# Four graph layers on one core: the tail of the neighbour maximum, with x fetched again, row minima, sums and statistics placed otherwise

## The reference, cut to what matters

```python
# x: (8192, 128) float32; adj: (8192, 8192) int32 of 0 and 1, symmetric, ones on the diagonal
def _L0_gnn_ref(X, adj):            # maximum over the neighbours, feature by feature
    neg = finfo(float32).min
    vals = max over j of where(adj[i, j] != 0, X[j, :], neg)
    return where(any(adj[i] != 0), vals, 0)

x = _layernorm(x + _L0_gnn_ref(x, adj))        # layer 0
x = _layernorm(x + attention_1(x, W1, a1, adj)) # layers 1 to 3: masked softmax attention
x = _layernorm(x + attention_2(adj, x, W2, a2))
x = _layernorm(x + attention_3(x, adj, W3, a3))
```

## Time and profile before

| what | value |
|---|---|
| median of three runs | 5988.77 us (5978.95 to 5993.84) |
| profiled execution: time / span | 6010.32 us / 6008.3 us |
| mean granted TensorE clock | 0.922 of full speed |
| busy share: PE, DVE, ACT, POOL | 84%, 79%, 34%, 20% |
| last `take_top` (L571) ends | 2253.55 us |
| first instruction of layer 1 on VectorE (L930) | 2316.70 us |

### The profile page before, as it was taken

One profiled execution on the slowest core, in us unless ns is written; L12 is line 12 of the kernel. 1 busy time (PEld: TensorE's weight loads), 2 busy tenths in 40 slices (PEclk: granted clock), 3 DMA queues, 4 the chain that ended last, 5 costly groups with the idle time before them and its releaser, 6 DMA issues. The chain is left out here.

```text
span 6008.3 us, 91716 instructions
## 1 busy us (share of the span) xinstructions
PE 5075.2 (84%) x24003; PEld 2392.2 (40%) x24113; DVE 4748.3 (79%) x8829; ACT 2028.6 (34%) x2862; POOL 1186.8 (20%) x1368
## 2 busy tenths in 40 slices
PE   4777767667677674899999999979999998999999
PEld 3333333333333332344444444435444445444444
DVE  6676766667666665699989998988888886888888
ACT  3444444444444441555555555510000001000000
POOL 5555454454444540000000000000000000000000
PEclk6888888888888885999999999998999998999999
DMA  7555555555555522011111111011222211221211
GB/s 256 191 189 190 188 187 180 178 189 187 184 185 181 184 94 85 29 43 44 44 43 43 44 44 44 29 44 63 72 76 74 73 49 71 74 82 67 89 60 35
DMA packets 149498, 628.30 MB, mean 105 GB/s; under 512 B 29360, under 2 KB 37936, under 8 KB 91632
## 3 DMA queue, kind: packets, MB, share of 16 engines
q1 hardware_dynamic: 78432, 482.58, 23.0%
q0 software_dynamic: 33744, 73.21, 4.1%
q10 hardware_dynamic: 36864, 67.13, 3.2%
HBM read 551.42 MB, written 75.56 MB: 104 GB/s over the span
## 5 line engine op out<-in xcount | busy, mean ns | idle before, releaser
L1258 PE MATMUL bank<-w,GX 128*128 128x512 f32 x6144 | 2777.6, 597 | 41.9 <-DVE w L1489 22.3
L1258 PEld LDWEIGHTS bank<-w,GX 128*128 128x128 f32 x6144 | 1145.6, 190 | 1398.2 <-issue 1340.4
L1503 DVE SCALAR_TENSOR_TENSOR w<-q,E,m 128x512 f32<-128x512 f32 x2048 | 1455.0, 758 | 170.0 <-PE bank L1258 92.0
L306 POOL DMA_INDIRECT ring<-x_ext,idx x1051 | 1030.4, 980 | 1098.1 <-DVE X L560 338.4
L450 PE MATMUL sums<-lone,xs 128*128 128x512 fp8e4 x3000 | 852.3, 427 | 300.9 <-DVE top L548 204.3
L548 DVE TENSOR_TENSOR top<-top,sums 128x1024 f32<-128x1024 f32 x484 | 589.8, 1219 | 645.2 <-remote 378.2
L375 ACT ACTIVATE stage<-tp 128x1024 fp8e4<-128x1024 uint16 x512 | 523.9, 1025 | 1089.9 <-remote 634.7
L1478 DVE SCALAR_TENSOR_TENSOR u<-theta,E,m 128x512 fp8e4<-128x512 f32 x1024 | 765.9, 749 | 98.3 <-issue 84.9
L1322 ACT ACTIVATE above<-bank,offset 128x512 fp8e4<-128x512 f32 x1024 | 649.0, 684 | 529.3 <-PE bank L1187 527.0
L1489 DVE SCALAR_TENSOR_TENSOR w<-q,E,u 128x512 f32<-128x512 f32 x1024 | 760.6, 744 | 74.9 <-PE bank L1258 74.8
L450 PEld LDWEIGHTS sums<-lone,xs 128*128 128x128 bf16 x3000 | 295.2, 106 | 827.4 <-issue 619.0
(11 more groups left out here) (231 smaller groups left out, 3018.2 us busy)
## 6 DMA issues: line engine op xcount, KB each, us to landing
adjb<-in_adj SPq DMA_DIRECT2D x256, 1024.0 KB
m<-mask_t SPq DMA_DIRECT2D x192, 1024.0 KB, 4.9
mask_t<-stage ACTq DMA_DIRECT2D x256, 256.0 KB
ring<-x_ext,idx POOLq DMA_INDIRECT x1051
out<-X SPq DMA_DIRECT2D x16, 256.0 KB, 2.4
Wn<-in_L_gnn_W SPq DMA_DIRECT2D x3, 64.0 KB, 1.9
A<-in_L_gnn_a SPq DMA_DIRECT2D x6, 0.5 KB, 2.1
X<-in_x SPq DMA_DIRECT2D x4, 0.5 KB, 22.3
```

The costliest lines, as they stand in the source:

```text
L306: pool.indirect_dma_start(ring[:, s, :], None, x_ext, bass.IndirectOffsetOnAxis(ap=idx[:, k, s:s + 1], axis=0)).then_inc(done, 16)
L1258: last = nc.tensor.matmul(acc[b][:, :], GX[:, j, :], w[:, j % WR, :], start=(j == 0), stop=(j == T - 1))
L1503: nc.vector.scalar_tensor_tensor(out=w[:, j % WR, :], in0=q, scalar=E[:, j:j + 1], in1=m[:, b, j, :], op0=ALU.max, op1=ALU.mult).then_inc( ...
```

## The change

- SyncE fetches x a second time as soon as the last adjacency tile has been turned, into `adjb` (`x_again`); `xin` and `bn0` go.
- The row minima of quads 0 to 14 are taken one quad at a time, one behind each of pairs 8 to 22 of the last quad; that of quad 15 behind the last `take_top`.
- GpSimd adds `x_again` to quads 0 to 14 of `nm`, one instruction a quad, behind its last gather; VectorE adds quad 15.
- The 64 `bn_stats` and 64 `bn_aggr` come before the branch, in the same block. ScalarE makes the flag of the reduced value. `first_norm` and its block go; the product with the 0/1 flag, with another sum and another set of statistics, stands in the branch that is not taken.
- The fallback's `tmp` moves from `adjb` to the second half of `stage[:, 0]`; `lowest` is a part of `codes`, `bn` a part of `keys`.

```diff
+LOWEST_AT = 8
+    nohas = found
-        tmp = adjb[:, :, :].rearrange("p h n -> p (h n)").bitcast(F32)[:, 0:FJ * F]
+        tmp = stage[:, 0, :, :].rearrange("p a b -> p (a b)").bitcast(F32)[:, FJ * F:2 * FJ * F]
+        x_again = adjb[:, :, :].rearrange("p h n -> p (h n)").bitcast(F32).rearrange("p (t f) -> p t f", f=F)
+        lowest = codes[:, 0:T]
+        bn = keys[:, 0:6 * T].rearrange("p (t s) -> p t s", s=6)
...
+            sp.wait_ge(transposed, T * 8)
+            sp.dma_start(x_again, x.rearrange("(t p) f -> p t f", p=P)).then_inc(x_back, 16)
             sp.wait_ge(flag_ready, 1)
...
             report()
+            pool.wait_ge(x_back, 16)
+            for quad in range(NC - 1):
+                at = slice(quad * TC, (quad + 1) * TC)
+                pool.wait_ge(rows_step, quad + 1)
+                nc.gpsimd.tensor_tensor(out=nm[:, at, :], in0=nm[:, at, :], in1=x_again[:, at, :], op=ALU.add).then_inc(x_added, 1)
             pool.wait_ge(missed_ready, 1)
...
                 act.wait_ge(stage_out[q], NC // 2 * STORES * 16)
+            act.wait_ge(missed_shared, 1)
+            nc.scalar.activation(flag[:, :], missed_all[:, :], ACT.Copy).then_inc(flag_ready, 1)
...
+            def lowest_of(quad):
+                at = slice(quad * TC, (quad + 1) * TC)
+                rows_done.did(nc.vector.tensor_reduce(lowest[:, at], nm[:, at, :], axis=AXX, op=ALU.min))
+            def between(n):
+                if n == LOWEST_AT:
+                    dve.wait_ge(top_used, NC - 1)
+                    dve.wait_ge(lower_free, T - TC + 1)
+                    dve.wait_ge(rest_free, T - TC + 1)
+                if LOWEST_AT <= n < LOWEST_AT + NC - 1:
+                    lowest_of(n - LOWEST_AT)
+            def row_statistics():
+                rows_done.settle()
+                dve.wait_ge(x_added, NC - 1)
+                for t in range(T):
+                    rows_done.did(nc.vector.bn_stats(bn[:, t, :], nm[:, t, :]))
+                rows_done.settle()
+                for t in range(T):
+                    rows_done.did(nc.vector.bn_aggr(stats[:, t, :], bn[:, t, :]))
+                rows_done.settle()
...
                     if quad is not None:
                         pair(quad * 32 + 8 * k + e, 8 * k + e, quad == NC - 1)
+                    if quad == NC - 1:
+                        between(8 * k + e)
...
-            dve.wait_ge(lower_free, T + 1)
-            dve.wait_ge(rest_free, T + 1)
             merge(NC - 1)
             take_top(NC - 1)
             dve.wait_ge(top_used, NC)
-            lowest = junk
-            steps.do(nc.vector.tensor_reduce(lowest, nm[:, :, :], axis=AXX, op=ALU.min))
             steps.did(nc.vector.scalar_tensor_tensor(out=due[:, :], in0=due[:, :], scalar=TOP_BIT, in1=found[:, :], op0=ALU.mult, op1=ALU.not_equal))
+            lowest_of(NC - 1)
+            rows_done.settle()
+            dve.wait_ge(x_back, 16)
+            last = slice(T - TC, T)
+            rows_done.did(nc.vector.tensor_tensor(out=nm[:, last, :], in0=nm[:, last, :], in1=x_again[:, last, :], op=ALU.add))
...
             nc.vector.tensor_reduce(missed[:, :], due[:, :], axis=AXX, op=ALU.max).then_inc(missed_ready, 1)
-            dve.wait_ge(missed_shared, 1)
-            nc.vector.tensor_copy(flag[:, :], missed_all[:, :]).then_inc(flag_ready, 1)
+            steps.do(nc.vector.tensor_scalar(nohas[:, :], deg[:, :], 0.0, None, ALU.is_equal))
+            row_statistics()
             dve.wait_ge(flag_ready, 1)
...
-            neighbour_max(...)
-            first_norm(nc, x, X, deg, nohas, stats)
+            neighbour_max(...)
```

More of the change, by code:

```diff
@@ L208, in neighbour_max @@
         x_copied = sem("x_copied")
+        x_back = sem("x_back")
+        rows_step = sem("rows_step")
+        x_added = sem("x_added")
         split = sem("split")
@@ L571, in take_top @@
                 nc.vector.tensor_tensor(out=tiles, in0=tiles, in1=turned_ps, op=ALU.max).then_inc(top_used, 1)
+            rows_done = Steps(dve, rows_step)
+            def lowest_of(quad):
[17 more added lines that the diff above has]
+                rows_done.settle()
             def phase(t, k, extracts=True, finishes=True, quad=None, tops=True):
@@ L704, in _ @@
             dve.wait_ge(top_used, NC)
-            lowest = junk
-            steps.do(nc.vector.tensor_reduce(lowest, nm[:, :, :], axis=AXX, op=ALU.min))
+            steps.settle()
+            side.settle()
             steps.did(nc.vector.scalar_tensor_tensor(out=due[:, :], in0=due[:, :], scalar=TOP_BIT, in1=found[:, :], op0=ALU.mult, op1=ALU.not_equal))
+            lowest_of(NC - 1)
[3 more added lines that the diff above has]
+            rows_done.did(nc.vector.tensor_tensor(out=nm[:, last, :], in0=nm[:, last, :], in1=x_again[:, last, :], op=ALU.add))
             steps.do(nc.vector.scalar_tensor_tensor(out=lowest, in0=lowest, scalar=0.0, in1=deg[:, :], op0=ALU.is_le, op1=ALU.mult))
@@ L743, in _ @@
                     hold(dve, fb_adj_used, t + 2)
-def first_norm(nc, x, X, deg, nohas, stats):
-    with ExitStack() as ctx:
-        sem = SEMS[0]
-        bn = ctx.enter_context(nc.sbuf_tensor("bn0", [P, T, 6], F32))
-        xin = ctx.enter_context(nc.sbuf_tensor("xin", [P, T, F], F32))
-        x_in, step, bn_done, ag_done = sem("x_again"), sem("step0"), sem("bn_done"), sem("ag_done")
-        block = ctx.enter_context(nc.Block())
-        @block.sync
-        def _(sp):
-            sp.dma_start(xin[:, :, :], x.rearrange("(t p) f -> p t f", p=P)).then_inc(x_in, 16)
-        @block.vector
-        def _(dve):
-            s = Steps(dve, step)
-            s.do(nc.vector.tensor_scalar(nohas[:, :], deg[:, :], 1.0, None, ALU.min))
-            s.do(nc.vector.tensor_tensor(out=X[:, :, :], in0=X[:, :, :], in1=nohas[:, :].unsqueeze(2).to_broadcast([P, T, F]), op=ALU.mult))
-            s.do(nc.vector.tensor_scalar(nohas[:, :], nohas[:, :], -1.0, 1.0, ALU.mult, ALU.add))
-            dve.wait_ge(x_in, 16)
-            s.do(nc.vector.tensor_tensor(out=X[:, :, :], in0=X[:, :, :], in1=xin[:, :, :], op=ALU.add))
-            for t in range(T):
-                nc.vector.bn_stats(bn[:, t, :], X[:, t, :]).then_inc(bn_done, 1)
-            dve.wait_ge(bn_done, T)
-            for t in range(T):
-                nc.vector.bn_aggr(stats[:, t, :], bn[:, t, :]).then_inc(ag_done, 1)
-            dve.wait_ge(ag_done, T)
+                rows_done.did(nc.vector.tensor_scalar(lowest, nohas[:, :], -1.0, 1.0, ALU.mult, ALU.add))
+                rows_done.settle()
+                rows_done.did(nc.vector.tensor_tensor(out=nm[:, :, :], in0=nm[:, :, :], in1=lowest.unsqueeze(2).to_broadcast([P, T, F]), op=ALU.mult))
+                rows_done.settle()
+                rows_done.did(nc.vector.tensor_tensor(out=nm[:, :, :], in0=nm[:, :, :], in1=x_again, op=ALU.add))
+                row_statistics()
 def attention_layer(nc, layer, W, a_src, a_dst, mask_t, X, nohas, stats, rstd, ident, lastrow, dest, out=None):
```

## The result

The changed kernel takes 5957.78 us (median of 5 executions, 5947.05 to 5960.98); the kernel before took 5987.64 us beside it (5 executions, 5978.95 to 5993.84). The ratio is 0.9949, 95% interval 0.9938 to 0.996: **29.9 us less**. The forecast was 5955.9 us, 32.9 less. The profiled execution took 5960.48 us, its span is 5957.5 us, its mean granted TensorE clock 0.928.

The account below looks back on a forecast made before the run. The prediction took a plain chain on VectorE, 63.15 us behind take_top, as the bound; 39.7 less 3.3 (minima) less 3.5 (collisions) gave 32.9 us off 5988.8, so 5955.9 us, range 5944 to 5974.

Parts of the forecast that it names:

- The chain: From the end of take_top to layer 1: 23.4 us in place of 63.15, 39.7 us less.
- the jump: VectorE's branch passing over 130 more instructions behind the statistics: 1.0 us for a code fetch, bounds 0 and 2.
- Ten minima: Minima between pairs 13 and 23 on VectorE: 3.3 us late at pair 23, bounds 0 and 10.35.
- Collisions of folds and sums: VectorE's folds of ring meeting GpSimd's sums: half of nine lose 0.78 us each, 3.5 us, bounds 0 and 11.7.
- Five minima for nothing: Minima behind pairs 8 to 12, ahead of the 5.64 us wait in front of pair 13: cost nothing.
- The fetch: Second fetch of x, issued at about 2157 us: some 22 us long, landing near 2180, cost 0.
- GpSimd's sums: Fifteen sums of 1.155 us from 2216.56, after 9.19 idle, ending at about 2243; their own length hidden.
- Rival 4: GpSimd's sums set the end: cost starts at 3.1 us each; at 6.6 us each the time is 6008 us; 3%.
- The drain: GpSimd's 8.4 us drain behind its reduction at the block's end: covered by VectorE's statistics, costing nothing.
- Rival 1: Drain belongs to the block's end, not the reduction, and is uncovered: 6.85 to 8.4 us lost, 5964 us; 8%.
- Rival 3: TensorE's clock falls to the 1.2 GHz level for pairs 14 to 31: 22.7 us come back, 5979 us; 4%.
- another layout of code: An example of effects the prediction could not see that would make the kernel slower: 1%.

Follow-up runs that it names:

- second set: Follow-up runs e6 to e9, on a chip of their own, where the kernel before stands at 5457.75 us (9 executions).
- e7: Changed kernel with 230 repeated waits, never executed, in VectorE's fallback branch, and a few on other engines; 5436.71 us, 0.9962 of before.
- e10: As e7 but with 266 waits instead of 230, 18 instructions more in VectorE's list; 5479.77 us (1 execution).
- e3: Changed kernel without the minima of quads 0 to 14, GpSimd's sums no longer held for them; 5433.08 us (1 execution).
- e9: Changed kernel with no edit, run again on another chip; 5437.01 us (5 executions), 0.9965 of before.
- e4: Changed kernel with the 128 statistics instructions moved behind the branch into a block of their own; 5510.62 us (1 execution).
- e2: Changed kernel with all 64 tiles' sums on VectorE in one instruction behind the last take_top, none on GpSimd; 5432.86 us (1 execution).
- e1: Kernel before with no edit, profiled a second time; 5464.39 us (1 execution).
- e5: Kernel before with GpSimd's reduction over partitions replaced by a copy; 5456.79 us (1 execution).
- e6: Changed kernel with x fetched twice, one behind the other, into the same place; 5432.28 us (1 execution).
- e8: Changed kernel with minima, GpSimd's sums and checks moved, 64 bn_aggr made six instructions, and 460 waits padding the branch; 5427.0 us, 0.9942 of before.

## Why the prediction was right

The forecast of 5955.9 us stands against 5957.78, inside the range, and faster by 0.5%. The mechanism, a plain chain of which 40 us go, was right. That the total came within 2 us is in part luck: the same change brings 20.7 us in the second set, and several terms below are off in ways that the first comparison hides or evens out. By its own steps:

- **The chain.** 23.4 forecast, 22.44 measured; 39.7 less, 40.7 measured. The one term that was off is the jump, put at 1.0 (bounds 0 and 2): it cost 0.4 in the changed kernel (0.6 from branch to drain, 0.2 before), and 2.5 more, outside the bounds, in e7 and e10, whose branch is longer still. 130 more instructions could be passed for next to nothing, 244 could not.
- **Ten minima.** 3.3 forecast, 3.8 by e3 against e9, 4.8 against e4.
- **Collisions of folds and sums.** 3.5 forecast, as half of nine folds losing 0.78 each; the four rows grew by 3.63, but as seven folds losing 0.52 on average, so the number is right by another mix. e2 has 4.9 to 5.9 for all that the sums did to pairs 13 to 23. The two terms together: 6.8 forecast, 6.9 in the first pair of traces. By e2 and e3 it would be 8.7 to 10.7. The kernel before itself takes 21.8 us in this stretch in e1 and 18.2 in e5, so the split into two terms is good to a couple of us, no better, and the 6.9 of one pair of traces is no closer confirmation than that. The Trainium skill (SBUF — State Buffer, "Who interferes with whom") spares instructions with one SBUF input, and the trace agrees: pairs and minima kept their 1.21 and 0.68 us beside the sums.
- **Five minima for nothing.** This rested on the wait of 5.64 us ahead of pair 13, and it holds where that wait is. In the first pair of traces pairs 8 to 12 take 19.5 and 19.7 us: the five minima fill VectorE's idle time, which falls from 10.2 to 7.7 us. The wait itself stayed (it is 6.39 after, and ends with `remote`, for something that the profile doesn't name); it was the idle time between the pairs that shrank. On the chips of the other sets the wait is missing, and the five cost 2.0 us, in every kernel that has them. The prediction called itself wrong if pairs 0 to 12 shift. They did, by 5.6 us the other way in the first pair, all of it ahead of pair 8 where no minimum stands, and the reason for that stays open.
- **The fetch.** Hidden, as forecast; even two are (e6).
- **GpSimd's sums.** 1.155 forecast, 1.269 measured (1.978 at most), done 15 us ahead of `take_top`. Rival 4, which needed 3.1 us each to cost anything, was far off. They began with 1.62 us of idle time, not 9.19.
- **The drain.** Covered, as forecast. The reason was half wrong: it doesn't belong to the reduction (e5). Rival 1 was right that it doesn't belong to the reduction and wrong about the consequence: the drain began at 2237.7, when GpSimd's own list had ended, and not at the barrier at 2256.2. e4 puts the cover's worth at 7.3.
- **TensorE's clock.** The mean granted clock is 0.88 in pairs 13 to 23, against 0.91 before in the earlier trace rows, a little lower, and 0.98 from 2220 to 2234.5. Rival 3, half the clock for 18 pairs, didn't come about.
- **What had no step.** The layers take 3691.6, 3689.5 and 3693.0 us in the three traces in which they are the layers of before (the first, e1, e5), 3691.7 to 3699.9 in the changed kernel and those near it (e4 and e10 apart): perhaps 3 to 4 us more on average. Since the one changed kernel has both 3691.7 and 3699.9, even that isn't shown. The 33.8 us of the change's own stretches less 4 would make the 29.9 of the medians, but this is a sum that fits and no proof. I had left 1% for "another layout of code". As a mechanism it is real and can be ten times as large (e10, e4); that it costs the changed kernel anything is argued only, and e7 speaks against the simple form of it. It is also open why the change brings 29.9 us in the first comparison and 20.7 in the second set. By the traces nearly all of it lies between pair 0 and the end of `take_top`, where the changed kernel takes 0.9 us more than before in the first pair (91.2 against 90.3) and 9.0 more in the second set (e9 83.1, e1 74.1). The five minima are 2 of these 8. The largest part is the 5.8 us ahead of pair 8, by which the first trace of before, a single one, was the longer.

## What to carry to other kernels

A chain on one engine behind a stage's last wait is worth its full length, and can be priced from single rows. Work moved out of it into a stretch without idle time is given back there, so look for the places where the engine waits for another (e8 took 7 us from the order alone). Ask too whether such a wait will be there in every run: the one ahead of pair 13 was missing on three chips. A wait at the end of a block is cheapest where its engine can start it early, under another's work. When code grows in a branch that is never taken, time what lies behind it too: put the branch's work in a loop, and try one or two lengths.

## What the hardware showed that I had not expected

- GpSimd's drain at the end of the neighbour maximum takes 8.15 to 8.41 us with a reduction as its last instruction and with a copy of 0.19 us.
- 18 instructions never executed, ahead of the layers in VectorE's list, make these 43.4 us longer (3692.7 to 3736.1), with twelve waits of 7.0 to 7.7 us that end in nothing the profile names.
- A jump over 114 instructions more costs 2.5 us (22.44 to 24.91), though the 130 that the change itself added cost only 0.4.
- The same program runs up to the last quad in 1636 us in the later sets instead of 2163, and the layers in the same time (3689.5 and 3691.6). The mean granted clock is 0.962 instead of 0.922. In the slower trace VectorE stands 369 us in 111 waits ahead of `top` that end in `remote`, for something that the profile doesn't name, and the faster one has none (waits up to the last quad, first comparison, before):

```profile
DVE top L548 <- remote: 369.2, 111, 11.6
```
